# The order of work within one step of a Performer attention loop: transposes of the query features before or after the context and output products

## The reference, cut to what matters

```python
def _softmax_kernel(data, proj, is_query):
    ratio = proj.shape[0] ** (-0.5)
    dn = data.shape[-1] ** (-0.25)
    dash = jnp.einsum('bhnd,md->bhnm', data * dn, proj)
    diag = 0.5 * dn ** 2 * jnp.sum(data * data, axis=-1, keepdims=True)
    if is_query:
        stab = jnp.max(dash, axis=-1, keepdims=True)
    else:
        stab = jnp.max(dash, axis=(-2, -1), keepdims=True)
    return ratio * (jnp.exp(dash - diag - stab) + EPS)
...
qp = _softmax_kernel(q, proj, True)
kp = _softmax_kernel(k, proj, False)
k_sum = jnp.sum(kp, axis=2)
d_inv = 1.0 / jnp.einsum('bhnm,bhm->bhn', qp, k_sum)
context = jnp.einsum('bhnm,bhnd->bhmd', kp, v)
out = jnp.einsum('bhnm,bhmd,bhn->bhnd', qp, context, d_inv)
return out.transpose(0, 2, 1, 3).reshape(b, n, N_HEADS * D_HEAD) @ Wo + bo
```

## Time and profile before

| | |
|---|---|
| runs | 2237.42, 2234.69, 2235.38 us; median 2235.38 us |
| profiled execution | 2230.61 us; first to last instruction 2228.7 us |
| TensorE | busy 1923.6 us (86%), mean granted clock 0.936 of 2.4 GHz |
| VectorE, ScalarE, GpSimd | busy 738.4, 399.5, 651.4 us |
| the attention loop | 975.0 us (first K) to 1202.2 us (last O read) |

### The profile page before, as it was taken

How to read it: one execution, slowest core, us unless ns; L and a number is a source line. 1 busy time by engine, 2 the same in 40 slices (tenths; PEclk the granted TensorE clock), 3 DMA queues, 4 the chain that set the end, 5 groups by cost and what they waited for, 6 DMA issues and landing times. The chain is left out here.

```text
span 2228.7 us, 22977 instructions
## 1 busy us (share of the span) xinstructions
PE 1923.6 (86%) x9082; PEld 1278.4 (57%) x9082; DVE 738.4 (33%) x1422; ACT 399.5 (18%) x721; POOL 651.4 (29%) x553
## 2 busy tenths in 40 slices
PE   4999999889887999999799588999989999999900
PEld 2465455445345774477676355776467787787700
DVE  5963123342251225434543344121001111111156
ACT  0000000011010110046564331100012121121132
POOL 0767821200003777778840000024001001001020
PEclk9999999999898999889899799999989999999955
DMA  9552142705001434232201122724158888888341
GB/s 339 143 133 51 2 132 56 207 30 231 33 1 55 141 89 119 61 83 53 56 17 53 77 87 76 312 57 105 38 212 335 325 333 333 322 339 332 130 105 46
DMA packets 116115, 314.90 MB, mean 141 GB/s; under 512 B 68361, under 2 KB 70996, under 8 KB 103892
## 3 DMA queue, kind: packets, MB, share of 16 engines
q1 hardware_dynamic: 30131, 228.09, 28.0%
q0 software_dynamic: 71120, 52.45, 10.6%
q10 hardware_dynamic: 14786, 33.29, 4.1%
HBM read 271.98 MB, written 41.31 MB: 141 GB/s over the span
## 5 line engine op out<-in xcount | busy, mean ns | idle before, releaser
L1830 PEld LDWEIGHTS bank<-picked_t,wring 128*128 128x128 f32 x2560 | 291.9, 194 | 10.3 <-issue 9.1
L1830 PE MATMUL bank<-picked_t,wring 128*128 128x128 f32 x2560 | 292.1, 277 | 0.8 <-DVE picked_t L1866 0.8
L320 PE MATMUL bank<-wring,ln_buf 128*125 128x512 f32 x480 | 207.6, 593 | 1.6 <-DVE ln_buf L623 0.7
L506 POOL DMA_INDIRECT table_d<-wring x85 | 173.7, 2043 | 109.0 <-issue 77.0
L320 PEld LDWEIGHTS bank<-wring,ln_buf 128*125 128x125 f32 x480 | 89.6, 188 | 115.3 <-issue 113.9
L1851 PE MATMUL bank<-wring,unit_t 128*128 128x512 f32 x320 | 148.0, 605 | 7.1 <-DVE unit_t L1872 7.1
L336 PE MATMUL bank<-x_buf,wring 128*128 128x312 f32 (+1 forms) x512 | 136.6, 430 | 13.7 <-PEq L953 13.7
L1933 POOL TENSOR_TENSOR unit_sq<-unit_t 128x512 f32<-128x512 f32 x20 | 20.8, 1040 | 426.5 <-DVE unit_t L1872 426.5
L1075 POOL DMA_INDIRECT score_d<-wring x90 | 116.8, 1298 | 70.1 <-DMA score_d<-wring 48.3
L336 PEld LDWEIGHTS bank<-x_buf,wring 128*128 128x128 f32 x512 | 97.7, 191 | 52.6 <-issue 15.2
L1061 POOL DMA_INDIRECT wring<-xr_d,wring x85 | 115.6, 1360 | 25.9 <-issue 24.1
(11 more groups left out here) (351 smaller groups left out, 2802.2 us busy)
## 6 DMA issues: line engine op xcount, KB each, us to landing
wring<-in_experts SPq DMA_DIRECT2D x60, 2048.0 KB, 8.4
wring<-in_L_Ws SPq DMA_DIRECT2D x6, 2048.0 KB, 24.3
b_b<-in_expert_b ACTq DMA_DIRECT2D x22, 512.0 KB, 8.1
routed_d<-out_rows ACTq DMA_DIRECT2D x20, 512.0 KB, 8.4
routed_d<-blank SPq DMA_DIRECT2D x1, 8192.0 KB, 46.2
table_d<-eq_buf SPq DMA_DIRECT2D x2, 3072.0 KB, 29.3
score_d<-no_edge SPq DMA_DIRECT2D x2, 3072.0 KB, 30.8
wring<-table_d POOLq DMA_DIRECT2D x10, 610.4 KB, 7.1
```

The lines of the kernel that those rows point to most:

```text
L320: ins = pe.matmul(bank[0:R, :], act_t[:, k, tok(t)], w[:, k * HALF:(k + 1) * HALF], start=(k == 0), stop=(k == chunks - 1))
L506: pool.indirect_dma_start(out=tables_d[b % 2], out_offset=bass.IndirectOffsetOnAxis(ap=edge_at[:, b:b + 1], axis=0), in_=edge_sums[:, b, : ...
L1830: ins = pe.matmul(bank[:, c * BLK:(c + 1) * BLK], w[:, k * HALF + c * P:k * HALF + (c + 1) * P], picked_t[:, s, k, :], start=(k == 0), sto ...
```

## The change

In the TensorE stream of the loop, the block that holds T(u-6) moves from the end of the step to a place right behind Q(u-5), ahead of C(u-1) and O(u-8). Its instructions and its waits are the same. No other engine's code changes.

```diff
                         pe.matmul(banks[1 + q % 2][0:R, 0:M], q1_t[p0:p0 + DH, h // 2, tok(t)], proj[p0:p0 + DH, :],
                                   start=True, stop=True).then_inc(hsem["q_prod"], 1)
+                    q = u - Q_LAG - 1
+                    if 0 <= q < UNITS:
+                        pe.wait_ge(hsem["q_exp"], q + 1)
+                        if q >= 1:
+                            pe.wait_ge(hsem["q_feat"], q)
+                        if q == 0:
+                            pe.wait_ge(features_set, 2)
+                        for c in range(3):
+                            ins = pe.transpose(banks[3][0:MC, c * R:(c + 1) * R], qf[:, q % 2, c * MC:(c + 1) * MC],
+                                               ident[0:R, 0:R])
+                        ins.then_inc(hsem["q_turned"], 1)
                     k = u - 1
                     if 0 <= k < UNITS:
...
                         ins.then_inc(hsem["q_used"], 1)
-                    q = u - Q_LAG - 1
-                    if 0 <= q < UNITS:
-                        pe.wait_ge(hsem["q_exp"], q + 1)
-                        if q >= 1:
-                            pe.wait_ge(hsem["q_feat"], q)
-                        if q == 0:
-                            pe.wait_ge(features_set, 2)
-                        for c in range(3):
-                            ins = pe.transpose(banks[3][0:MC, c * R:(c + 1) * R], qf[:, q % 2, c * MC:(c + 1) * MC],
-                                               ident[0:R, 0:R])
-                        ins.then_inc(hsem["q_turned"], 1)
```

## The result

The changed kernel takes 2287.73 us (median of 4 runs, 2284.48 to 2292.62) against 2235.73 us: 52.0 us slower, ratio 1.0234 with a 95% interval of 1.0214 to 1.0253. The profiled executions took 2288.1 and 2230.61 us, 57.5 apart; the one of before lies 5 us under its median, so the medians are the better measure of the whole and the traces of its parts.

A forecast was written before the change was run, and what follows sets the result against it. TensorE was taken as the bound at 2.35 us a loop step, plus gather waits. Steps of 3.58 us add 63.2 us to the profiled 2230.61, giving 2293.8; 4.8 to the median gives 2298.6 us, range 2280 to 2335.

The forecast's parts named there:

- What bounds the loop: Loop before the change: TensorE at 2.35 us a step, and one group of gathers per 24.7 to 25.9 us.
- `q_feat` wait: T's wait for line 1463 of the same step, behind line 1455 and K: step grows 1.23 to 3.58 us.
- T to what follows: In the new step, start of T to start of C: taken as 0.46 us, 0.41 in the lower bound.
- C to O: In the new step, start of C to start of O: taken as 0.61 us.
- O to the next K: In the new step, start of O to start of the following K: taken as 0.69 us.
- What the slower step gives back: Gather waits at VectorE's line 1084 in steps 22, 30, 38 and 46 vanish; 26.6 us of disturbances before.
- The ends of the loop: Steps 7 to 79 pay; nothing after the loop absorbs it; last three steps may save up to 1 us.
- wait for `q_exp`: T's wait for line 1476 of the step before, moved with it behind Q: costs nothing.
- The sum: Whole kernel: 61.9 us more over 72 loop steps plus 1.23 for step 79, +63.2 us.
- The clock: Rival: TensorE's clock falls to 1.2 GHz in the loop, 2355 us (third of steps) to 2467 (all); chance 0.13.
- Hidden by the gathers: Rival: gather pace hides most added wait up to step 46, steps under 3.09 us; +14 us, 2249; chance 0.06.
- Faster: Rival: earlier T lets ScalarE catch up in four steps stalled on `q_exp`; 5.2 us less, 2230; chance 0.02.

The follow-up runs named there:

- e5: Kernel before the change, with the scatters of groups 10 to 17 issued two groups later in GpSimd's stream: 2210.97 us, ratio 0.9896.
- e1: Changed kernel with ScalarE's line 1463 moved ahead of line 1455 in its step: 2242.75 us, ratio 1.0043 to the kernel before.
- e4: Kernel before the change, with T put between C and O, ahead of O instead of ahead of C: 2251.63 us, ratio 1.0078.
- e9: Changed kernel with the scatters two groups later in GpSimd's stream: 2291.16 us, ratio 1.0254 to the kernel before.
- e7: Changed kernel with line 1463 ahead of line 1455 on ScalarE and scatters two groups later: 2223.34 us, ratio 0.9950 to the kernel before.

## Why the prediction was right

**What bounds the loop** was read rightly: TensorE at 2.35 us a step, and the gathers. e5 shows both, 2.40 us a step on the mean once most of the gather waits are gone.

**The `q_feat` wait** is the mechanism, shown by e1, e4 and e9: shorten it on the other engine and the time comes back, put one block under it and a part comes back. The sum of the step was 3.58 and measured 3.51. Three terms share the error: T to what follows 0.36 (0.46 taken, and 0.41 in the lower bound), C to O 0.54 (0.61 taken, in the lower bound too), O to the next K 0.77 (0.69 taken). Two of them lie outside the bounds given, and the whole stayed inside because the third erred the other way. K to line 1455 was 0.75 and line 1455 to T 1.09, as the rows of before said. The time from one block to the next thus depends on which two they are.

**What the slower step gives back**: the four gather waits vanished, GpSimd's loads of group 17 started at 1107.37 (1108.10 before) and its last scatter at 1190.56, all clear of the loop's end, as worked out. The hidden part was put at 26.6 us; it is 23 by the traces and 28 by the medians (e9).

**The ends of the loop** were in part not right. A wait for `q_exp` was put at nothing, and up to step 84 that holds: TensorE's only idle time of that kind is 1.0 us ahead of the last T. Behind step 79 the prediction allowed up to 1 us less; it was 2.9 more, of which 1.15 is step 79 itself, as forecast. The rest, 1.7 us, is a wait left out of the sum: line 1463 also waits for `q_used`, so for an O, which now ends each step. The prediction said that line 1463 would run ahead there; it ran behind that O, and T behind it, as in step 80 (the products of the O of step 79 end at 1246.44):

```profile
1246.54 0.57 ACT L1463 ACTIVATE qf_t<-bank,eps_ratio 89x375 f32<-89x375 f32 x1 [1.22 <-PE bank L1260]
...
1247.25 0.53 PE L1235 MATMUL bank<-ident,qf 125*89 125x125 f32 x3 [0.17 <-ACT qf_t L1463]
```

Steps 80 to 83 are some 0.2 us longer each for it, and what follows the last Q is 1.0 us longer.

**The sum**: +63.2 predicted, +52.0 measured (47.8 to 56.6 by the interval). The loop of the trace grew by 61.0, which looks closer than it was. Steps 7 to 79 came to 57.4, 5.7 less than the 63.1 of the sum, because a step was 3.50 us on the mean and not 3.58. The 1.7 us behind them, which the sum left out, and the 1.9 us of the longer start at 1.2 GHz, which the change didn't cause, made up for most of that: this part of the agreement is luck. The other 9 us between 61.0 and 52.0 lie outside the loop and in the step from single executions to medians: the profiled execution of before was 5 us under its median, and the stages outside the loop vary. Adding the loop's growth to the profiled time and then moving to the median was sound in form, but it rests on a single execution.

**The rivals.** The clock did not fall: 1.00 from step 7 to the loop's end. Hidden by the gathers: true in part and only for short waits, as e1 shows, where 0.20 us a step cost 9.6 us in the whole (12.0 in the traced steps) and not 14. The limit of 3.09 us a step that this rival was given is too high: e4's steps of 2.96 us met no gather wait. Faster: the program excludes it, since line 1455 stands ahead of line 1463; with that order turned round (e1, e7) early T was still no gain, 12.4 us slower than e5 where the gathers are out of the way.

## What to carry to other kernels

In a loop over several in-order engines, look for each wait at what the signalling instruction stands behind on its own engine. Here a wait moved forward by 1.3 us closed a chain within one step, from TensorE to ScalarE and back, and cost 1.15 us a step; moving the signalling operation ahead of the one that closes the chain brought that down to 0.20. Look also at the granted clock of both executions before putting a difference down to the change: here 1.9 us at the loop's start were a longer time at 1.2 GHz. And a stall elsewhere, here VectorE's wait for gathers, hides part of such a loss. Removing the stall was worth more than any order of TensorE's stream tried here: scatters issued two groups later in GpSimd's stream made the kernel 22.8 us faster than before.

## What the runs showed of the hardware

With a pause of 1.1 us in every step of 3.51 us, TensorE kept 2.4 GHz for 250 us on end (granted clock 1.00, busy 171.6 of 250 us). At the loop's start it was granted 1.2 GHz for 13.7 us in some executions and 17.1 us in others, with either order of T; in the kernel before it was busy for 9.70 of the 9.70 us from 977.7 to 987.4 and still at 0.50.

The time from the start of one block of small fp32 products to the next depends on the neighbour: C's six MATMUL records took 0.77 us behind K and Q and 0.70 behind T, and O to K took 0.77 where O to T took 0.69.

In the changed kernel a scatter between two gathers took 1.5 us of GpSimd's stream in most cases (1092.10 to 1093.61). One that follows another waits for its landing, as the program demands, and in the last group they came every 2.8 to 2.9 us (1182.00, 1184.88, 1187.76, 1190.56). That fits the finding that moving scatters out of the gathers' way has a best size (2211 us at two groups later, 2221 at three, 2234 with all at the end), where the score loads waited 4.6, 18.0 and 33.4 us for the last scatter.
